# Motif terms of a convolution network: the large loads and stores move from SP's queue to GpSimd's

## The chip, the cores and the metric

One core of a Trainium2 chip runs the whole program. The metric is the device time in microseconds, the median of several executions. The engines are TensorE (PE), VectorE (DVE), ScalarE (ACT), GpSimd (POOL) and SyncE (SP). SP and GpSimd each issue DMA transfers, on queues of their own (q1 "hardware dynamic" and q0 "software dynamic" in the profile); 16 DMA engines serve both.

## The reference

For each of two images of 128 x 128 positions and 96 channels, a group-normalised copy of `x` goes through a channel attention (1x1 and 3x3 depthwise convolutions, softmax over channels), whose result is added to `x`. Then comes the part that matters here, on a group-normalised copy read as planes:

```
motif_nn = take_along_axis(motif, u_max[..., None, None], axis=3)   # one neighbour channel per (group, tap)
term = floor(motif * motif_nn * c_max[..., None, None] / Cg)
out_ser = motif * batch_mask + term          # batch_mask: 0 for image 0, 1 for image 1
...
for k in range(K * K):
    ki, kj = (k // K, k % K)
    out = out.at[:, :, :, ki:ki + Hm, kj:kj + Wm].add(ser2[:, :, :, k])
x = x + out
```

`motif` holds nine shifted views of each plane. The partner plane of a plane depends on data (`u_max`, by nearest neighbour over the Gram matrices), so it has to be gathered.

## The kernel before

The program runs per image: `attention`, `motif_grams` (normalise, write the planes `f` to DRAM, Gram matrices, partner choice) and `motif_terms` (from line 1028). Only `motif_terms` is changed. While it works on image 0 it also loads image 1 in pieces (`x_next`) and takes its statistics, since the next attention needs them.

`motif_terms` has the 128 planes on the partitions and works on N = 8 blocks of R = 16 rows. Per block there are nine tap steps (`sh` 0 to 8), in the order of `steps`: blocks go in pairs, and the steps of a pair alternate, (0,0), (1,0), (0,1), (1,1) and so on, so a pair takes 18 steps and an image 72. In this document product n, step n and move n carry the same number n from 0 to 71.

Per step, VectorE multiplies the plane's rows by the partner's rows (`product`, L1097, into `prod`); ScalarE rounds the scaled product (L1279, L1284); VectorE marks where rounding overshot (`overshoot`, L1213, two steps later); TensorE adds both into the accumulators in PSUM at the tap's shift (L1301, L1305). After a block's ninth tap `finish` (L1222) adds the accumulators to `x1c`. For image 1 `own_patches` (L1238) adds the block's own nine-fold patches at tap 3; for image 0 `stats_share` (L78) takes a share of the next image's statistics from step 19 on.

Transfers, with four buffers (`SLOTS`) each for fc, near, near2 and x1c:

- `fc<-f_planes` (`load_rows`, 768 KB): a block's planes. Blocks 0 and 1 at the start, block i+2 at tap 5 of block i.
- `x1c<-x_planes` (`load_rows`, 768 KB): the rows to which the result is added. Blocks 0 and 1 at tap 1, block i+2 at tap 4 of block i.
- `out<-x1c` (`store`, 768 KB): block i-2 at tap 2 of block i, the last two at the end, waited for at L1160.
- `x_next<-in_x` (`load_next`, 384 KB): 16 pieces, from step 7, four in every 13 steps, image 0 only.
- `near<-f_planes,index` (`gather`, L1166): the partner planes, by index from DRAM, two gathers per block (`near` for the first tap, `near2` for the partner's neighbour), issued by GpSimd. Those of blocks 0 and 1 at the start, those of block i+2 at taps 1 and 3 of block i.
- `near<-near` (L1137, about 100 KB): at each tap from 1 on one plane in eight gets a new partner, copied from near2 to near. The move of step n waits for product n-2 and, at tap 1, for the gather of near2; product n waits for it. These are the 128 moves of the run.

SP issues all of these but the gathers, from one written-out order: at each step the move first, then what else is due. GpSimd's own program has only two memsets and the gathers; the first four depend on the index that VectorE computes, the next four (blocks 2 and 3) wait for nothing, and later ones wait for the last products of the block whose buffer they take (L1077, through `product_made`). `on_pool` is False throughout, so GpSimd makes no product.

Of the kernel before, what the change touches and what calls it, by code (L numbers as in the profile page):

```python
# [33 lines left out]
B, H, W, C = 2, 128, 128, 96  # L34
# [10 lines left out]
KK = 9  # L45
# [7 lines left out]
QROWS = 32  # L53
NQ = H // QROWS
# [973 lines left out]
def motif_terms(nc, b, k, x, f_dram, x1_dram, out, gram_sems):  # L1028
# [3 lines left out]
    R = 16  # L1032
    N = H // R
    SLOTS = 4
# [3 lines left out]
    with ExitStack() as ctx:  # L1038
# [4 lines left out]
        fc = sb("fc", [P, SLOTS, R * C], F32)  # L1043
        x1c = sb("x1c", [P, SLOTS, R * C], F32)
# [4 lines left out]
        if b + 1 < B:  # L1049
            x_next = sb("x_next", [P, 2 * QROWS, C], F32)  # L1050
            next_in = [sem(f"next_in{j}_") for j in range(2)]
            next_stats = sem("next_stats")
# [9 lines left out]
        stored, near_in, near2_in, fc_in, x1_in = ([sem(f"{n}{j}_") for j in range(SLOTS)]  # L1062
                                                   for n in ("stored", "near_in", "near2_in", "fc_in", "x1_in"))
# [3 lines left out]
        number = {st: n for n, st in enumerate(steps)}  # L1067
        on_pool = [False for i, sh in steps]

        STATS_PER, STATS_AT, LOAD_AT = 13, 19, 7  # L1070
# [4 lines left out]
        def product_made(eng, n):  # L1075

            eng.wait_ge(prod_p if on_pool[n] else prod_v, sum(p == on_pool[n] for p in on_pool[:n + 1]))  # L1077

        def product_inputs(eng, n):

            i, sh = steps[n]
            s = i % SLOTS
            if sh == 0:
                eng.wait_ge(near_in[s], 16 * (i // SLOTS + 1))
                eng.wait_ge(fc_in[s], 16 * (i // SLOTS + 1))
                eng.wait_ge(edged, 2 if i == N - 1 else 1)
            else:
                eng.wait_ge(moved[i % 2], 16 * (8 * (i // 2) + sh))
            if n >= PRODS:
                eng.wait_ge(over_done, n - PRODS + 1)  # L1090

        def product(vec, n):
            i, sh = steps[n]
            s, (dy, dx) = i % SLOTS, TAPS[sh]
            fv = fc[:, s, :].rearrange("p (r c) -> p r c", c=C)[:, :, dx:dx + WM]
            nv = near[:, s, :].rearrange("p (r c) -> p r c", c=C)[:, 2 - dy:2 - dy + R, 0:WM]
            return vec.tensor_tensor(prod[:, n % PRODS], fv, nv, ALU.mult)  # L1097

        def run(i):

            a = (first_row(i) - (R * i - 2)) * C
            return slice(a, a + (last_row(i) - first_row(i)) * C + WM)

        out_p = out[b].rearrange("y x c -> y (x c)")
        block = ctx.enter_context(nc.Block())

        @block.sync
        def _(sp):
            def load_rows(dst, src, i, sem_):
                sp.dma_start(dst[:, i % SLOTS, :], src[:, R * i * C:(R * i + R) * C]).then_inc(sem_[i % SLOTS], 16)  # L1110

            def load_next(q, piece):

                cols, slot = QROWS // 4, QROWS * (q % 2)
                if q >= 2 and piece == 0:
                    sp.wait_ge(next_stats, q - 1)
                sp.dma_start(x_next[:, slot + cols * piece:slot + cols * (piece + 1), :],
                             x[b + 1][:, QROWS * q + cols * piece:QROWS * q + cols * (piece + 1), :]
                             ).then_inc(next_in[q % 2], 16)

            def store(i):
                sp.wait_ge(out_ready, i + 1)
                sp.dma_start(out_p[:, R * i * C:(R * i + R) * C], x1c[:, i % SLOTS, :]
                             ).then_inc(stored[i % SLOTS], 16)

            if b + 1 < B:
                for s_ in gram_sems.values():
                    sp.sem_clear(s_)
            for i in range(2):
                load_rows(fc, f_dram, i, fc_in)  # L1130
            for n, (i, sh) in enumerate(steps):
                if sh >= 1:

                    if sh == 1:
                        sp.wait_ge(near2_in[i % SLOTS], 16 * (i // SLOTS + 1))
                    product_made(sp, n - 2)
                    sp.dma_start(near[MC - sh:P:MC, i % SLOTS, run(i)], near2[MC - sh:P:MC, i % SLOTS, run(i)]  # L1137
                                 ).then_inc(moved[i % 2], 16)
                if sh == 5 and i + 2 < N:
                    if i >= 2:  # L1140
                        product_made(sp, number[(i - 2, KK - 1)])
                        product_made(sp, number[(i - 2, KK - 2)])
                        if b == 1:
                            sp.wait_ge(fold, i - 1)
                    load_rows(fc, f_dram, i + 2, fc_in)
                if i >= 2 and sh == 2:
                    store(i - 2)
                if sh == 1 and i < 2:
                    load_rows(x1c, x1_dram, i, x1_in)
                q, part = (n - LOAD_AT) // STATS_PER, (n - LOAD_AT) % STATS_PER  # L1150
                if b + 1 < B and 0 <= q < NQ and part in (0, 3, 6, 9):
                    load_next(q, part // 3)
                if sh == 4 and i + 2 < N:
                    if i >= 2:
                        sp.wait_ge(stored[(i + 2) % SLOTS], 16 * ((i + 2) // SLOTS))
                    load_rows(x1c, x1_dram, i + 2, x1_in)
            for i in range(N - 2, N):
                store(i)
            for j in range(SLOTS):
                sp.wait_ge(stored[j], 16 * (N // SLOTS))  # L1160

        @block.gpsimd
        def _(pool):
            def gather(i, second):
                s = i % SLOTS
                pool.indirect_dma_start(  # L1166
                    (near2 if second else near)[:, s, run(i)], None, f_dram.rearrange("y (e o) -> (y e) o", o=1),
                    bass.IndirectOffsetOnAxis(ap=index[:, second, i:i + 1], axis=0)
                ).then_inc((near2_in if second else near_in)[s], 16)


            nc.gpsimd.memset(near[:, 0, 0:2 * C], 0.0).then_inc(edged, 1)
            pool.wait_ge(indexed, 1)
            for second in range(2):
                gather(0, second)
                gather(1, second)
            for n, (i, sh) in enumerate(steps):
                if sh in (1, 3) and i + 2 < N:
                    if sh == 1 and i >= 2:
                        product_made(pool, number[(i - 2, KK - 1)])  # L1180
                        product_made(pool, number[(i - 2, KK - 2)])
                    if sh == 1 and i + 2 == N - 1:
                        nc.gpsimd.memset(near[:, (i + 2) % SLOTS, R * C:NR * C], 0.0).then_inc(edged, 1)
                    gather(i + 2, sh // 2)
                if on_pool[n]:
                    product_inputs(pool, n)
                    product(nc.gpsimd, n).then_inc(prod_p, 1)

        @block.vector
        def _(dve):  # L1190
# [172 lines left out]
```

## Time and profile before

| what | value |
|---|---|
| median of 3 runs | 1781.23 us (1780.07 to 1782.25) |
| the profiled execution, its own time | 1786.56 us |
| its span | 1784.6 us |
| PE busy | 1497.0 us (84%) |
| DVE busy | 990.3 us (55%) |
| ACT busy | 735.0 us (41%) |
| POOL busy | 317.9 us (18%) |
| granted TensorE clock, mean | 0.928 |
| q1 (SP's transfers) | 116.10 MB |
| q0 (GpSimd's transfers) | 27.49 MB |

All times of rows are microseconds from the span's start, in the one profiled execution. The shares are means over very different stages. The motif terms of image 0 run from about 608 to 908 us, those of image 1 from about 1485 to the end. An instruction of VectorE starts in the record while the one before it still drains, so neighbours overlap by some 0.1 us. In a timeline the square brackets hold the idle time ahead of an instruction and what ended it. A granted clock of 1.0 is 2.4 GHz, 0.5 is 1.2 GHz.

### The profile page before, as it was taken

To read this page: it belongs to the slowest core of one execution; us is meant where nothing else is said; L and a number is where in the kernel's file an instruction comes from. 1 tells how busy PE (TensorE), PEld (TensorE's weight loads), DVE (VectorE), ACT (ScalarE), POOL (GpSimd) and SP (SyncE) were. 2 spreads that over 40 slices of the span, in tenths; PEclk is the share of its full clock that TensorE was granted. 3 is DMA by queue.
4 is the path that set the end of the run, shared out by engine and by line. 5 is a ranking of instruction groups with operands and counts; after the bars stand their busy time and mean duration, and the time that the engine had idled before them with its cause. 6 is when DMAs were issued, how large, how long until landed. Compare 5 with 4: busy or idle time off the path is not lost. (4 is left out here: it accounts for less than half of the span.)

```text
span 1784.6 us, 40475 instructions
## 1 busy us (share of the span) xinstructions
PE 1497.0 (84%) x16955; PEld 1257.2 (70%) x16955; DVE 990.3 (55%) x1537; ACT 735.0 (41%) x769; POOL 317.9 (18%) x254
## 2 busy tenths in 40 slices
PE   0699999799299488988949999988975993898998
PEld 0699999699299344544539999988974991454554
DVE  7333332123743379999962333321346415999998
ACT  0133332100154178877812332330003532888886
POOL 2222222000531202100022222220005302024000
PEclk9999999899699689999979999998996996999999
DMA  5111111010003364462112222201010216362511
GB/s 190 35 35 34 37 35 28 13 74 38 36 2 143 116 234 166 151 215 74 38 63 60 61 60 59 61 16 49 38 73 1 85 61 234 99 198 78 169 59 52
DMA packets 50959, 145.99 MB, mean 82 GB/s; under 512 B 12311, under 2 KB 33421, under 8 KB 48143
## 3 DMA queue, kind: packets, MB, share of 16 engines
q1 hardware_dynamic: 46192, 116.10, 20.4%
q0 software_dynamic: 4608, 27.49, 4.3%
q8 instruction: 133, 2.18, 0.5%
q14 instruction: 26, 0.21, 0.0%
HBM read 72.69 MB, written 37.75 MB: 62 GB/s over the span
## 5 line engine op out<-in xcount | busy, mean ns | idle before, releaser
L1301 PE MATMUL acc<-rnd,ident 128*128 128x376 f32 x1152 | 405.5, 497 | 24.7 <-ACT rnd L1284 24.7
L599 PE MATMUL ps_a<-wa,xa 128*128 128x192 f16 x2304 | 406.2, 248 | 14.0 <-DMA xc<-low 14.0
L600 PE MATMUL ps_a<-wb,xb 128*128 128x192 f16 x2304 | 405.6, 248 | 0.0
L1301 PEld LDWEIGHTS acc<-rnd,ident 128*128 128x128 f32 x1152 | 224.6, 199 | 153.1 <-ACT rnd L1284 26.1
L1279 ACT ACTIVATE rnd_m<-prod,plus_round,scale 128x1504 f32<-128x1504 f32 x144 | 236.0, 1639 | 121.2 <-DVE prod L1097 114.8
L1097 DVE TENSOR_TENSOR prod<-fc,near 128x1504 f32<-128x1504 f32 x144 | 246.6, 1713 | 39.5 <-DMA near<-near 25.2
L1213 DVE SCALAR_TENSOR_TENSOR over<-prod,scale,rnd 128x1504 bf16<-128x1504 f32 x144 | 255.4, 1776 | 0.9 <-PE acc L1305 0.9
L599 PEld LDWEIGHTS ps_a<-wa,xa 128*128 128x128 f16 x2304 | 227.0, 99 | 15.5 <-issue 11.7
L468 DVE TENSOR_TENSOR qk<-ps_a,qk 128x384 f16<-128x384 f32 x128 | 71.4, 557 | 295.4 <-ACT squares L549 295.4
L1284 ACT ACTIVATE rnd<-rnd_m,minus_round 128x1504 f32<-128x1504 f32 x144 | 223.1, 1550 | 25.9 <-PE acc L1305 20.8
L600 PEld LDWEIGHTS ps_a<-wb,xb 128*128 128x128 f16 x2304 | 227.3, 99 | 1.0
L599 PE MATMUL ps_a<-wfa,xa 128*128 128x96 f16 x2232 | 220.1, 206 | 0.0
L600 PE MATMUL ps_a<-wfb,xb 128*128 128x96 f16 x2232 | 219.2, 206 | 0.0
L428 POOL TENSOR_TENSOR sq_sum<-sq_sum,squares 128x384 f32<-128x384 f32 x128 | 127.5, 996 | 408.9 <-ACT squares L549 408.9
L600 PEld LDWEIGHTS ps_a<-wfb,xb 128*128 128x128 f16 x2232 | 193.3, 98 | 0.1
L599 PEld LDWEIGHTS ps_a<-wfa,xa 128*128 128x128 f16 x2232 | 193.1, 98 | 0.0
L545 ACT ACTIVATE qk<-ps_a 128x384 f16<-128x384 f32 x128 | 62.9, 491 | 280.7 <-PE ps_a L602 280.7
L1305 PE MATMUL acc<-over,minus_ident 128*128 128x376 bf16 x576 | 119.1, 330 | 31.3 <-DVE over L1213 31.0
L516 DVE SCALAR_TENSOR_TENSOR img<-ps_a,img 128x384 f32 (+1 forms) x64 | 35.7, 557 | 179.8 <-PE ps_a L602 157.9
L1305 PEld LDWEIGHTS acc<-over,minus_ident 128*128 128x128 bf16 x576 | 50.1, 99 | 120.4 <-DVE over L1213 81.5
L127 ACT ACT_TABLE_LOAD x3 | 3.8, 1283 | 285.6 <-PEq L301 261.2
L951 DVE TENSOR_SCALAR turned_lo<-ps_m 126x768 f16<-126x768 f16 x102 | 56.4, 558 | 106.8 <-PE ps_m L855 106.8
(227 smaller groups left out, 2030.1 us busy)
## 6 DMA issues: line engine op xcount, KB each, us to landing
x_planes<-img SPq DMA_DIRECT2D x8, 1536.0 KB, 5.6
f_planes<-img SPq DMA_DIRECT2D x8, 1536.0 KB, 11.1
fc<-f_planes SPq DMA_DIRECT2D x16, 768.0 KB, 4.6
x1c<-x_planes SPq DMA_DIRECT2D x16, 768.0 KB, 4.8
out<-x1c SPq DMA_DIRECT2D x16, 768.0 KB, 3.3
near<-near SPq DMA_DIRECT2D x96, 107.9 KB, 2.2
xb<-xa SPq DMA_DIRECT2D x64, 97.5 KB, 2.1
img<-in_x SPq DMA_DIRECT2D x4, 1536.0 KB, 12.6
```

The lines of the kernel that those rows point to most:

```text
L428: nc.gpsimd.tensor_tensor(sq_sum[:, :], sq_sum[:, :], squares[:, s, :], ALU.add).then_inc(sq_added, 1)
L468: nc.vector.tensor_tensor(qk[:, s, :, 2 * C:4 * C], ps[s][:, 0:4 * C].rearrange("p (r o) -> p r o", r=2), qk[:, s, :, 0:2 * C], ALU.subtra ...
L545: nc.scalar.activation(qk[:, s, :, 0:2 * C], ps[s][:, 0:4 * C].rearrange("p (r o) -> p r o", r=2), ACT.Copy)
L599: nc.tensor.matmul(out, xa[:, row, dx:dx + W], wa[:, t, :], start=(t == 0), stop=False)
L600: nc.tensor.matmul(out, xb[:, row, dx:dx + W], wb[:, t, :], start=False, stop=False)
L951: last = nc.vector.tensor_scalar(columns(turned_lo[q % 2], col), six(ps_lo[u % 2]), 2.0, None, ALU.mult)
L1097: return vec.tensor_tensor(prod[:, n % PRODS], fv, nv, ALU.mult)
L1213: nc.vector.scalar_tensor_tensor(over[:, n % 2], prod[:, n % PRODS], scale[:, sh:sh + 1], rnd[:, n % RNDS], ALU.mult, ALU.is_lt).then_inc( ...
L1279: nc.scalar.activation(rnd_m[:, n % 2], prod[:, n % PRODS], ACT.Identity, bias=k["plus_round"][:, 0:1], scale=scale[:, sh:sh + 1]).then_in ...
L1284: nc.scalar.activation(rnd[:, n % RNDS], rnd_m[:, n % 2], ACT.Identity, bias=k["minus_round"][:, 0:1]).then_inc(rnd_done, 1)
L1301: nc.tensor.matmul(o(m), k["ident"][:, :], rnd[:, n % RNDS, BR * m:BR * m + BR, :], start=False, stop=False, skip_group_check=True)
L1305: last = nc.tensor.matmul(o(m), k["minus_ident"][:, :], over[:, n % 2, BR * m:BR * m + BR, :], start=False, stop=(sh == KK - 1), skip_grou ...
```

## The change

`load_rows`, `load_next` and `store` are moved, as they are, from the program of SP to that of GpSimd, with the calls of them. SP keeps the semaphore clears and the moves. GpSimd issues the first two fc loads ahead of its memset and its first gathers. In each step it now issues the gathers that are due, waits for product n-2, and then issues what SP issued behind its move. The waits for products that guarded the fc buffer's reuse are dropped for that one wait per step; the one for `fold` in image 1 stays. GpSimd waits for the last stores.

```diff
         @block.sync
         def _(sp):
-            def load_rows(dst, src, i, sem_):
-                sp.dma_start(dst[:, i % SLOTS, :], src[:, R * i * C:(R * i + R) * C]).then_inc(sem_[i % SLOTS], 16)
...
-            for i in range(2):
-                load_rows(fc, f_dram, i, fc_in)
             for n, (i, sh) in enumerate(steps):
...
-                if sh == 5 and i + 2 < N:
-                    if i >= 2:
-                        product_made(sp, number[(i - 2, KK - 1)])
-                        product_made(sp, number[(i - 2, KK - 2)])
-                        if b == 1:
-                            sp.wait_ge(fold, i - 1)
-                    load_rows(fc, f_dram, i + 2, fc_in)
-                if i >= 2 and sh == 2:
-                    store(i - 2)
-                if sh == 1 and i < 2:
-                    load_rows(x1c, x1_dram, i, x1_in)
...
-                if sh == 4 and i + 2 < N:
-                    if i >= 2:
-                        sp.wait_ge(stored[(i + 2) % SLOTS], 16 * ((i + 2) // SLOTS))
-                    load_rows(x1c, x1_dram, i + 2, x1_in)
-            for i in range(N - 2, N):
-                store(i)
-            for j in range(SLOTS):
-                sp.wait_ge(stored[j], 16 * (N // SLOTS))
 
         @block.gpsimd
         def _(pool):
...
+            for i in range(2):
+                load_rows(fc, f_dram, i, fc_in)
             nc.gpsimd.memset(near[:, 0, 0:2 * C], 0.0).then_inc(edged, 1)
             pool.wait_ge(indexed, 1)
...
                     gather(i + 2, sh // 2)
-                if on_pool[n]:
-                    product_inputs(pool, n)
-                    product(nc.gpsimd, n).then_inc(prod_p, 1)
+                if n >= 2:
+                    product_made(pool, n - 2)
+                if sh == 5 and i + 2 < N:
+                    if b == 1 and i >= 2:
+                        pool.wait_ge(fold, i - 1)
+                    load_rows(fc, f_dram, i + 2, fc_in)
+                if i >= 2 and sh == 2:
+                    store(i - 2)
+                if sh == 1 and i < 2:
+                    load_rows(x1c, x1_dram, i, x1_in)
+                q, part = (n - LOAD_AT) // STATS_PER, (n - LOAD_AT) % STATS_PER
+                if b + 1 < B and 0 <= q < NQ and part in (0, 3, 6, 9):
+                    load_next(q, part // 3)
+                if sh == 4 and i + 2 < N:
+                    if i >= 2:
+                        pool.wait_ge(stored[(i + 2) % SLOTS], 16 * ((i + 2) // SLOTS))
+                    load_rows(x1c, x1_dram, i + 2, x1_in)
+            for i in range(N - 2, N):
+                store(i)
+            for j in range(SLOTS):
+                pool.wait_ge(stored[j], 16 * (N // SLOTS))
```

## Rows read from the trace of the kernel before

**Rows 1.** Busy time by stretch: start and steady state of image 0; granted clock, DMA share, GB/s last

```profile
608.00:650.00 42.00, 21.48 (x59) 11.31 (x60) 21.78 (x26) 19.83 (x13) 10.09 (x9) 0.65 0.71 263
650.00:716.00 66.00, 61.48 (x222) 34.91 (x221) 66.00 (x51) 57.35 (x37) 11.32 (x4) 0.95 0.57 183
```

**Rows 2.** Waits of VectorE, whole run: total, times, longest

```profile
DVE prod L1097 <- DMA near<-near: 25.2, 7, 6.5
```

**Rows 3.** Timeline of VectorE, start of image 0: products 2, 3, 4 and 5

```profile
628.54 1.73 DVE L1097 TENSOR_TENSOR prod<-fc,near 128x1504 f32<-128x1504 f32 x1 [6.38 <-DMA near<-near]
...
633.99 1.73 DVE L1097 TENSOR_TENSOR prod<-fc,near 128x1504 f32<-128x1504 f32 x1 [2.03 <-DMA near<-near]
...
640.77 1.73 DVE L1097 TENSOR_TENSOR prod<-fc,near 128x1504 f32<-128x1504 f32 x1 [3.36 <-DMA near<-near]
...
644.11 1.72 DVE L1097 TENSOR_TENSOR prod<-fc,near 128x1504 f32<-128x1504 f32 x1
```

**Rows 4.** Timeline of SP's queue, start of image 0

```profile
610.22 0.80 SPq L1110 DMA_DIRECT2D fc<-f_planes  x2
622.47 0.60 SPq L1137 DMA_DIRECT2D near<-near  x1
623.13 0.56 SPq L1110 DMA_DIRECT2D x1c<-x_planes  x1
624.77 0.55 SPq L1137 DMA_DIRECT2D near<-near  x1
625.37 0.57 SPq L1110 DMA_DIRECT2D x1c<-x_planes  x1
```

**Rows 5.** DMA issues between 608 and 626: count, size, us to landing

```profile
x1c<-x_planes SPq DMA_DIRECT2D x2, 768.0 KB, 12.4
...
near<-near SPq DMA_DIRECT2D x1, 107.9 KB, 9.2
near<-near SPq DMA_DIRECT2D x1, 95.9 KB, 6.0
```

**Rows 6.** DMA issues of the whole run: median us to landing

```profile
x1c<-x_planes SPq DMA_DIRECT2D x16, 768.0 KB, 4.8
...
near<-near SPq DMA_DIRECT2D x96, 107.9 KB, 2.2
```

**Rows 7.** Busy time by stretch, two short stretches at image 0's start

```profile
612.00:618.00 6.00, 0.00 (x0) 0.00 (x0) 0.00 (x0) 0.00 (x0) 4.47 (x6) 0.50 0.98 403
...
636.00:642.00 6.00, 5.68 (x18) 2.97 (x17) 2.64 (x2) 2.94 (x2) 0.00 (x0) 0.90 0.46 156
```

**Rows 8.** Timeline of VectorE, image 1: products 2, 3, 4, and one at 1660

```profile
1504.47 1.73 DVE L1097 TENSOR_TENSOR prod<-fc,near 128x1504 f32<-128x1504 f32 x1 [6.51 <-DMA near<-near]
...
1509.88 1.73 DVE L1097 TENSOR_TENSOR prod<-fc,near 128x1504 f32<-128x1504 f32 x1 [1.99 <-DMA near<-near]
...
1515.65 1.72 DVE L1097 TENSOR_TENSOR prod<-fc,near 128x1504 f32<-128x1504 f32 x1 [2.35 <-DMA near<-near]
...
1660.68 1.72 DVE L1097 TENSOR_TENSOR prod<-fc,near 128x1504 f32<-128x1504 f32 x1 [2.62 <-DMA near<-near]
```

**Rows 9.** Timelines of GpSimd, then of VectorE beside its gathers

```profile
609.13 0.26 POOL L1172 MEMSET near<- 128x192 f32 x1 [53.57 <-POOLq L730]
...
613.67 0.94 POOL L1166 DMA_INDIRECT near<-f_planes,index  x1 [0.30 <-issue]
...
1565.91 3.03 POOL L1166 DMA_INDIRECT near<-f_planes,index  x1 [0.30 <-issue]
...
1628.75 15.57 POOL L1166 DMA_INDIRECT near<-f_planes,index  x1 [53.15 <-DVE prod L1097]
...
1568.05 1.78 DVE L1213 SCALAR_TENSOR_TENSOR over<-prod,scale,rnd 128x1504 bf16<-128x1504 f32 x1
...
1643.40 1.77 DVE L1222 TENSOR_TENSOR x1c<-x1c,acc 128x1536 f32<-128x1536 f32 x1
```

**Rows 10.** Timeline of SP's queue: the last two stores

```profile
1777.71 3.50 SPq L1123 DMA_DIRECT2D out<-x1c  x2
```

More of the change, by code:

```diff
@@ L1108, in _ @@
         def _(sp):
-            def load_rows(dst, src, i, sem_):
-                sp.dma_start(dst[:, i % SLOTS, :], src[:, R * i * C:(R * i + R) * C]).then_inc(sem_[i % SLOTS], 16)
[L1112 to L1124, printed above, removed]
             if b + 1 < B:
@@ L1138, in _ @@
                                  ).then_inc(moved[i % 2], 16)
-                if sh == 5 and i + 2 < N:
-                    if i >= 2:
-                        product_made(sp, number[(i - 2, KK - 1)])
-                        product_made(sp, number[(i - 2, KK - 2)])
-                        if b == 1:
-                            sp.wait_ge(fold, i - 1)
-                    load_rows(fc, f_dram, i + 2, fc_in)
-                if i >= 2 and sh == 2:
-                    store(i - 2)
-                if sh == 1 and i < 2:
-                    load_rows(x1c, x1_dram, i, x1_in)
-                q, part = (n - LOAD_AT) // STATS_PER, (n - LOAD_AT) % STATS_PER
-                if b + 1 < B and 0 <= q < NQ and part in (0, 3, 6, 9):
-                    load_next(q, part // 3)
-                if sh == 4 and i + 2 < N:
-                    if i >= 2:
-                        sp.wait_ge(stored[(i + 2) % SLOTS], 16 * ((i + 2) // SLOTS))
-                    load_rows(x1c, x1_dram, i + 2, x1_in)
-            for i in range(N - 2, N):
-                store(i)
-            for j in range(SLOTS):
-                sp.wait_ge(stored[j], 16 * (N // SLOTS))
         @block.gpsimd
@@ L1169, in gather, with load_rows, load_next, store @@
                 ).then_inc((near2_in if second else near_in)[s], 16)
+            def load_rows(dst, src, i, sem_):
+                pool.dma_start(dst[:, i % SLOTS, :], src[:, R * i * C:(R * i + R) * C]).then_inc(sem_[i % SLOTS], 16)
+            def load_next(q, piece):
+                cols, slot = QROWS // 4, QROWS * (q % 2)
+                if q >= 2 and piece == 0:
+                    pool.wait_ge(next_stats, q - 1)
+                pool.dma_start(x_next[:, slot + cols * piece:slot + cols * (piece + 1), :],
+                             x[b + 1][:, QROWS * q + cols * piece:QROWS * q + cols * (piece + 1), :]
+                             ).then_inc(next_in[q % 2], 16)
+            def store(i):
+                pool.wait_ge(out_ready, i + 1)
+                pool.dma_start(out_p[:, R * i * C:(R * i + R) * C], x1c[:, i % SLOTS, :]
+                             ).then_inc(stored[i % SLOTS], 16)
+            for i in range(2):
+                load_rows(fc, f_dram, i, fc_in)
             nc.gpsimd.memset(near[:, 0, 0:2 * C], 0.0).then_inc(edged, 1)
```

## The prediction

> **What bounds the kernel now.** The change touches one stage, the motif terms of each image, so I first asked the busy time by stretch how that stage runs. In steady state VectorE has no free time: 66.00 us of 66.00, and two of its products stand 3.34 us apart (640.77 to 644.11) [rows 1, 3]. In the first 42 us it is busy for only 21.78 us [rows 1]. The list of waits says on what: 25.2 us in 7 waits for a small move `near<-near`, the largest single releaser in the stage [rows 2]. So a gain can only come from those 25.2 us, a loss from anything that makes VectorE wait anew, or that lengthens a start or an end, where nothing covers it.
>
> The VectorE timeline of image 0 places three of the seven waits, before products 2, 3 and 4 (step numbers of the kernel): 6.38, 2.03 and 3.36 us [rows 3]. The SP timeline shows what lies between the moves: each of the first two is followed at once by a 768 KB load of x1c on the same queue [rows 4]. The DMA issues of this stretch give the landing times: 6.0 us for the first move, 9.2 for the second, and 12.4 for x1c loads that take 4.8 us in the whole run's median, where a move takes 2.2 [rows 5, 6]. The engines' share of busy time is 0.98 early in it, and only after 636 us does it fall to 0.46 [rows 7]: everything issued before that shares full DMA engines. Image 1 repeats the pattern (6.51, 1.99, 2.35 us) and has a seventh wait of 2.62 us at 1660 [rows 8].
>
> **The change, part by part.** Of SP's queue, 64 transfers go: 16 fc, 16 x1c, 16 stores and 16 x_next pieces, with their waits. SP keeps the 128 moves. GpSimd gets the 64 behind and between its 32 gathers, and a new wait at each step, for product n-2.
>
> *Moves 3 and 4 at the start.* Now move 3 stands behind x1c(0) and move 4 behind x1c(0) and x1c(1) in SP's queue. Afterwards SP's queue holds moves alone. GpSimd's queue holds fc(0), fc(1), four gathers, the fifth gather, x1c(0), the sixth gather, x1c(1); the gathers seven and eight now wait until step 6. Before product 4 that is 10 large transfers instead of 12, and the two taken out are the last. At some 2.1 us each (860 KB at the 403 GB/s of a full stretch [rows 7]) ten last 21 us, until about 633; move 4 is issued at the end of product 2, near 630, and product 4 needs it at 635. I take both later waits as gone: product 4 then follows product 2 by two steps of 3.33 us, at 628.54 + 6.66 = 635.2 instead of 640.77, **-5.6 us**; in image 1 at 1504.47 + 6.66 = 1511.1 instead of 1515.65, **-4.5 us** [rows 3, 8]. Bounds: 0 if moves wait as long as now, -10.1 for both. What is late next here is TensorE: its granted clock is 0.50, the 1.2 GHz level, before its first work of the stage, and 0.65 in the mean of the stretch [rows 1, 7]; I leave 1 us for that in the range.
>
> *Move 2* waits first for its gather and then 6.0 us for itself, with nothing ahead of it on its own queue [rows 4, 5]. What held it was the other queue's gathers, and those stand ahead of it still. I take 0; if its own queue being empty were to help, it could gain 6.0 - 2.2 = 3.8 us per image, 7.6 in all.
>
> *The wait at 1660.* GpSimd's gather of 1628.75 took 15.57 us, until VectorE's instruction at 1643.40 [rows 9], so three more gathers fell into 5 us, with two stores, and a move came late. After the change a wait for a product stands between gathers, so that they come a step apart. **-2.6 us**; 0 if the bunch forms again.
>
> *Starts.* GpSimd makes descriptors for 0.94 us before a transfer can begin (the undisturbed gather), SP's issue of a load returns in 0.57 [rows 4, 9]. In image 0 SP begins at 610.22, GpSimd at 609.13 already, and the two loads put 2 x 1.24 = 2.5 us of issuing ahead of the first gather, whose data stand behind these loads in any case: -0.2 us. In image 1, where SP doesn't clear semaphores first, +0.8. Together **+0.6 us**; bounds 0 and +2.5 (the gathers each 1.24 us later).
>
> *Ends.* Each image ends with a store whose landing nothing covers: issued at about 1780.9, with the end at 1784.6 [rows 10]. From GpSimd it starts about 0.9 us later (0.94 us of descriptors). Twice: **+1.8 us**, bounds 0.8 and 4. The Trainium skill (DMA: Bandwidth & Descriptors, Latency and other measured facts) has 1 us to the first byte from GpSimd against 0.6 from SP; by that the two ends would cost 0.8.
>
> *Steady state.* GpSimd gets 64 x (0.94 + 0.30) = 79 us of issuing over the two stages, SP loses about 35; neither is the bound. What hides it: per pair of blocks, 18 steps or 60 us and more, GpSimd has at most 10 large issues and, in image 0, some five x_next pieces. At the 3.03 us that a gather takes beside VectorE [rows 9] fifteen are 45 us. The tightest is fc, issued 8 steps (27 us) before its product. Behind each new wait for product n-2 stand later gathers: gather(4) is issued after product 17 and wanted at step 36, 19 steps. A store waits for VectorE's sum and holds the next issues for some 3 us; the x1c slot is wanted two steps behind. I take 0. If the cover goes, the price is in the third rival.
>
> Sum: -5.6 - 4.5 - 2.6 + 0.6 + 1.8 = -10.3 us. Against the profiled execution, 1786.56 us with a span of 1784.6, that is 1776.3. It ran 5.3 us above the median of the runs; on the median, 1781.23 - 10.3 = **1771 us**.
>
> **The rivals.**
>
> *More than forecast.* Move 2 is also set free: 7.6 us more, 1763 us. For it: its queue holds nothing else. Against: it holds nothing ahead of it now either.
>
> *Nothing.* The engines, not the queue, hold the moves; x1c(0) and x1c(1) on GpSimd's queue hold moves 3 and 4 just as long, and the bunch at 1660 forms again. Left are starts and ends: 1781.2 + 2.4 = 1783.6, within what a measurement of this kernel can tell from no change (0.2%, 3.6 us). For it: the share of 0.98, and move 2's 6.0 us. Against: move 3 took 3.2 us longer than move 2, with only a load of its own queue between them [rows 5].
>
> *Slower: GpSimd is held off by VectorE.* The gather of 15.57 us shows that this can be: it ended 0.92 us after VectorE began an instruction that reads the accumulators in PSUM (1643.40), while others ended about 0.9 us after a change of VectorE instruction (1568.94, with `over` begun at 1568.05) [rows 9]. So a gather wants a gap between VectorE's instructions with two inputs in SBUF, and sometimes gets none; the 0.9 us of descriptors then run beside them. Such a gather now has loads behind it. It decides when the delay reaches the 27 us of fc less about 5 for landing. In image 1 a gather at tap 3 could be held until VectorE runs dry of fc; then each pair costs about what a load takes behind a backlog, 12.4 us [rows 5], three pairs 37 us: 1771 + 37 = 1808. Against: eight gathers amid such streams took 3 to 4 us each, one 15.57; a direct load has no index to read; and the short own-patch instructions of image 1, one to four steps on, leave gaps. The Trainium skill (SBUF — State Buffer, SBUF: two separate sides) warns of just this: DMAs from GpSimd starve where VectorE holds the shared port. It names copies in fast modes for descriptors, and two-input instructions for GpSimd's reads; the rows agree with the second.
>
> **How the numbers follow.** The forecast has 0.60 (own range 1765 to 1777: the wait at 1660 may stay, TensorE may take 1 us, starts and ends may cost 3 more). More than forecast 0.12, nothing 0.14, slower 0.14, since loads from GpSimd beside this VectorE stream are in no row. The range takes the first three, 1763 to 1784. Faster by over 0.2%: 0.60 + 0.12 = 0.72; within: 0.14; slower: 0.14.
>
> **What the changed profile would show.** Right: waits of `prod` for `near<-near` fall from 25.2 us in 7 to about 12.9 in 2, both before product 2; moves 3 and 4 land within 7 us; the last store ends about 0.9 us later behind its sum. Wrong: VectorE waiting before products 3 and 4 as now; a wait of `prod` for `fc<-f_planes` or of `x1c` for `x1c<-x_planes`; direct issues on GpSimd of over 3 us; a move late in steady state behind a load.

## The result, and the profile after

The changed kernel takes 1784.01 us (median of 20 runs, 1781.34 to 1786.41) where the kernel before takes 1781.37 (20 runs, 1776.41 to 1784.56). The ratio is 1.0016, with an interval from 1.0009 to 1.0022: 2.6 us slower, less than the 3.6 us that I had named as telling from no change, but with 1 outside the interval. The forecast was 10 us faster. The median lies at the upper end of the range that the prediction gave, 1763 to 1784 us, and 0.01 us outside it, and the likeliest case is wrong.

The page of the changed kernel, its span, queues and DMA issues (q1 is fed by SP, q0 by GpSimd; the issues end with median us to landing):

```profile
span 1782.5 us, 40529 instructions
...
q1 hardware_dynamic: 36976, 72.06, 13.1%
q0 software_dynamic: 12800, 71.54, 11.6%
...
fc<-f_planes POOLq DMA_DIRECT2D x16, 768.0 KB, 5.5
x1c<-x_planes POOLq DMA_DIRECT2D x16, 768.0 KB, 5.9
out<-x1c POOLq DMA_DIRECT2D x16, 768.0 KB, 3.8
near<-near SPq DMA_DIRECT2D x96, 107.9 KB, 2.3
```

The change does what it says: loads and stores are GpSimd's, SP keeps the moves. Busy time by stretch of the changed kernel, the two stretches of [rows 1] with the same columns, and the waits of VectorE, total, times and longest:

```profile
608.00:650.00 42.00, 25.47 (x79) 13.90 (x80) 27.49 (x28) 25.76 (x17) 15.08 (x17) 0.71 0.85 299
650.00:716.00 66.00, 61.00 (x227) 35.18 (x225) 64.37 (x55) 56.16 (x36) 14.73 (x16) 0.97 0.56 181
```

```profile
DVE prod L1097 <- DMA near<-near: 16.8, 6, 6.7
DVE prod L1097 <- DMA near<-f_planes,index: 14.9, 4, 7.3
DVE part L88 <- PEq L1038: 9.0, 1, 9.0
```

VectorE is busy for 27.49 us of the first 42 where it was 21.78 [rows 1], and waits for moves for 16.8 us where it waited 25.2 [rows 2]. In the steady stretch it has lost what it had: 64.37 us of 66.00, where it was 66.00. And a third line has grown that had no part in the prediction: one wait of 9.0 us, in front of line 88, the first VectorE instruction behind the stage of image 0. In the kernel before this wait is 3.8 us.

The timeline of VectorE in the changed kernel, start of image 0 (products 2 to 5), answers to [rows 3]:

```profile
627.87 1.73 DVE L1097 TENSOR_TENSOR prod<-fc,near 128x1504 f32<-128x1504 f32 x1 [6.27 <-DMA near<-near]
...
631.21 1.72 DVE L1097 TENSOR_TENSOR prod<-fc,near 128x1504 f32<-128x1504 f32 x1
...
634.57 1.73 DVE L1097 TENSOR_TENSOR prod<-fc,near 128x1504 f32<-128x1504 f32 x1
...
637.91 1.72 DVE L1097 TENSOR_TENSOR prod<-fc,near 128x1504 f32<-128x1504 f32 x1
```

The waits before products 3 and 4 are gone and the one before product 2 stands as it was. Counted from the VectorE instruction that begins the stage (609.17 before, 608.45 after), product 4 begins at 26.12 us instead of 31.60, 5.5 earlier; in image 1 at 26.14 instead of 29.69, 3.55 earlier.

Now the end of image 0. Timeline of VectorE in the changed kernel: the last sum and the next instruction; then the timeline of GpSimd, its last store and its next instruction; then the rows of the block's end (line 1038) in this image, with count, shortest/median/longest ns and start:

```profile
902.27 1.75 DVE L1218 TENSOR_TENSOR x1c<-x1c,acc 128x1536 f32<-128x1536 f32 x1 [1.41 <-PE acc L1301]
913.06 0.49 DVE L88 TENSOR_REDUCE part<-stats 128x32 f32<-128x256 f32 x1 [9.03 <-PEq L1038]
```

```profile
904.32 0.53 POOL L1145 DMA_DIRECT2D out<-x1c  x1 [2.34 <-DVE x1c L1218]
913.02 0.53 POOL L396 MEMSET low<- 96x520 uint32 x1 [8.17 <-POOLq L1038]
```

```profile
L1038 POOLq DRAIN  x1: 4644/4644/4644, 908.1 to 908.1; - x1
```

The same places in the kernel before: the rows of line 1038 (both images) and VectorE's wait:

```profile
L1038 POOLq DRAIN  x2: 13791/21728/29665, 755.6 to 1631.9; - x2
...
L1038 SPq DRAIN  x2: 7/7/7, 911.0 to 1784.4; - x2
```

```profile
911.23 0.49 DVE L88 TENSOR_REDUCE part<-stats 128x32 f32<-128x256 f32 x1 [3.82 <-PEq L1038]
```

Every engine ends a block with a DRAIN, and the block is over when the last one is. Before, SP waited for the last landing and its own DRAIN took 7 ns; GpSimd's was long, 13.8 and 29.7 us, but began at 755.6 and 1631.9, over a hundred microseconds ahead of the end. Now GpSimd waits for the last landing, until 908.1, and then its DRAIN runs for 4.64 us with nothing beside it. The end of image 0 is 9.03 us instead of 3.82, the end of image 1 (end of the last sum to end of the span) 1782.5 - 1774.55 = 7.95 instead of 1784.6 - 1780.84 = 3.76.

**The ledger of the two profiled executions.** Stage start to the end of the last sum: image 0 from 298.24 to 295.57 us (-2.7), image 1 from 294.88 to 289.97 (-4.9). The two ends: +5.2 and +4.2. Together +1.8 us, which agrees with the 2.6 of the medians. (The two spans alone would say -2.1; but between them lie stretches that the change doesn't touch and that differ by 3.9 us, which is why I go by the stage.)

Of the 5.5 us that image 0 wins in its first four steps, 2.8 are lost again on the way. The timeline of VectorE in the changed kernel has these two waits, which stood nowhere before, and the timeline of GpSimd shows what lies ahead of the first:

```profile
711.88 1.72 DVE L1097 TENSOR_TENSOR prod<-fc,near 128x1504 f32<-128x1504 f32 x1 [1.63 <-DMA near<-near]
...
783.67 1.73 DVE L1097 TENSOR_TENSOR prod<-fc,near 128x1504 f32<-128x1504 f32 x1 [1.01 <-DMA near<-near]
```

```profile
699.18 0.53 POOL L1145 DMA_DIRECT2D out<-x1c  x1 [4.71 <-DVE x1c L1218]
699.70 0.55 POOL L1139 DMA_DIRECT2D x_next<-in_x  x1
700.55 1.05 POOL L1125 DMA_INDIRECT near<-f_planes,index  x1 [0.30 <-issue]
701.91 1.38 POOL L1125 DMA_INDIRECT near<-f_planes,index  x1 [0.30 <-issue]
```

A store that waits for VectorE's sum holds up what stands behind it, and then four large transfers leave within 4 us. That looks like the cause of the late moves; the experiment that was to show it didn't (below).

### The profile page after: what moved, and what is told of

Same layout as the page of the kernel before. It is cut to its first block and busy times, and to the rows that moved or that the text cites. A ratio compares the mean times of both kernels' runs of the same rounds, so it can differ in the third digit from the quotient of the medians.

```text
span 1782.5 us, 40529 instructions
## 1 busy us (share of the span) xinstructions
PE 1491.0 (84%) x16955; PEld 1253.3 (70%) x16955; DVE 990.3 (56%) x1537; ACT 735.3 (41%) x769; POOL 337.5 (19%) x318
## 5 line engine op out<-in xcount | busy, mean ns | idle before, releaser
L1097 DVE TENSOR_TENSOR prod<-fc,near 128x1504 f32<-128x1504 f32 x144 | 246.8, 1714 | 31.7 <-DMA near<-near 16.8
```

## The experiments

**What makes the end long.** There are three other ways of sharing the last two stores and the landing wait between SP and GpSimd; the rest of the changed kernel stays. First, both on SP (`last_store_sp` is `store` with a semaphore of its own, `last_stored`).

```diff
@@ changed kernel, SP, at its end
+            for i in range(N - 2, N):
+                last_store_sp(i)
+            for j in range(SLOTS):
+                sp.wait_ge(stored[j], 16 * (N // SLOTS - (j >= SLOTS - 2)))
+            sp.wait_ge(last_stored, 32)
@@ GpSimd, at its end
-            for i in range(N - 2, N):
-                store(i)
-            for j in range(SLOTS):
-                pool.wait_ge(stored[j], 16 * (N // SLOTS))
```

> The changed kernel, but the last two stores of each image and the wait for their landing are SP's again. By the profile of the changed kernel the time from the end of the last x1c sum to the next work grew at both image ends (3.82 to 9.04 us, and 3.76 to 7.95 us to the end of the span), 9.4 us together, where 1.8 was forecast. Theory A (GpSimd, once it has issued a DMA late, comes some 4 to 5 us late to the end of its block): both ends fall back to about 3.8 us and the kernel is 9.4 us faster than the changed one, about 6.8 us (0.4%) faster than before. Theory B (waiting for the landing on GpSimd is what is slow): the same here. Rival C (the changed kernel lost its start's gain in the steady state, the ends are an accident of one profile): within 2 us of the changed kernel.

Measured: 1774.16 us (1771.88 to 1775.39, 5 runs) against 1781.34 of the kernel before, ratio 0.9955, interval 0.9942 to 0.9967. That is 9.9 us less than the changed kernel. The rows of line 1038 and VectorE's wait behind image 0 in this kernel:

```profile
L1038 POOLq DRAIN  x2: 3170/3826/4481, 886.2 to 1752.0; - x2
...
L1038 SPq DRAIN  x2: 7/7/7, 907.6 to 1772.6; - x2
```

```profile
907.88 0.49 DVE L88 TENSOR_REDUCE part<-stats 128x32 f32<-128x256 f32 x1 [3.81 <-PEq L1038]
```

GpSimd's DRAIN is as long as ever, but begins at 886.2 and 1752.0, some 20 us ahead of the end. Both ends are back at 3.81 and 3.74 us. So all of the loss lies in the last two stores and their wait, and the rest of the change is worth -7.2 us.

The other two take one of the two parts each: the stores on GpSimd and the wait on SP, and the stores on SP and the wait on GpSimd.

```diff
@@ changed kernel, GpSimd, at its end
             for i in range(N - 2, N):
                 store(i)
-            for j in range(SLOTS):
-                pool.wait_ge(stored[j], 16 * (N // SLOTS))
@@ SP, at its end
+            for j in range(SLOTS):
+                sp.wait_ge(stored[j], 16 * (N // SLOTS))
```

> The changed kernel, GpSimd still issues the last two stores, but the wait for their landing is SP's. Theory A (GpSimd's late DMA itself holds GpSimd at the end of its block): the ends stay at about 9 and 8 us, the time is the changed kernel's within 1.5 us. Theory B (only GpSimd's wait for the landing is slow): the ends fall to about 4.7 us (3.8 and 0.9 for GpSimd's start of a DMA), 7.6 us faster than the changed kernel.

```diff
@@ changed kernel, SP, at its end
+            for i in range(N - 2, N):
+                last_store_sp(i)
@@ GpSimd, at its end
-            for i in range(N - 2, N):
-                store(i)
             for j in range(SLOTS):
-                pool.wait_ge(stored[j], 16 * (N // SLOTS))
+                pool.wait_ge(stored[j], 16 * (N // SLOTS - (j >= SLOTS - 2)))
+            pool.wait_ge(last_stored, 32)
```

> The changed kernel, the last two stores issued by SP, but GpSimd waits for their landing. Theory A (a late DMA of its own is what holds GpSimd): the ends fall to about 3.8 us, 9 us faster than the changed kernel. Theory B (GpSimd's wait for the landing is slow): the ends stay at 8 us or so, at most 2 us faster than the changed kernel.

Measured: stores on GpSimd, wait on SP 1779.47 us (11 runs, ratio 0.9990, 0.9981 to 0.9999), ends 6.44 and 5.73 us; stores on SP, wait on GpSimd 1782.74 (12 runs, ratio 1.0013, 0.9998 to 1.0028), ends 8.33 and 6.95. Line 1038 in the one, then in the other:

```profile
L1038 POOLq DRAIN  x2: 5226/5554/5882, 904.9 to 1773.5; - x2
L1038 SPq DRAIN  x2: 7/7/7, 908.7 to 1777.2; - x2
```

```profile
L1038 SPq DRAIN  x2: 122/122/123, 903.6 to 1774.3; - x2
L1038 POOLq DRAIN  x2: 3170/3826/4481, 906.7 to 1777.4; - x2
```

The kernel whose last stores SP issues, and for which only GpSimd waits, is nearly as slow as the changed one. Its ends exceed the 3.82 and 3.76 of before by 4.51 and 3.19 us, its DRAINs are 4.48 and 3.17: the whole excess is the DRAIN. It isn't the issue of the store, nor the wait in itself, but what GpSimd must still do once the wait is over. That refutes a store of GpSimd's own as the cause. With the wait on SP the DRAIN starts while the store is still under way (904.9), and part of it is covered. It is longer there than in the changed kernel, 5.88 and 5.23 us instead of 4.64 and 3.33, so the ends fell to 6.44 and 5.73 us and not to the 4.7 that was expected if the wait alone were slow.

**If it is the DRAIN, one more of them, placed earlier, should take it away** with every store and wait left on GpSimd:

```diff
@@ changed kernel, GpSimd, at its end
+            pool.drain()
             for i in range(N - 2, N):
                 store(i)
```

> The changed kernel with one more DRAIN on GpSimd, ahead of its last two stores of each image, where it waits for VectorE anyway. So far the DRAIN that ends GpSimd's block took 4.644 us in an image with 56 DMAs issued by GpSimd, 4.481 with 54, 3.988 with 48, 3.333 with 40, 3.170 with 38 and 2.680 with 32: 0.082 us for each DMA since the block began. Theory E (the DRAIN pays 0.082 us for each DMA since the last DRAIN): the last DRAIN falls to about 0.2 us, the ends from 9.03 and 7.95 us to about 4.6 and 4.8, and the kernel is some 7.5 us faster than the changed one, near 1776.5. Rival (a fixed cost of leaving a block late, or one by the whole block's DMAs): ends and time stay as in the changed kernel.

Measured: 1774.70 us (1773.56 to 1777.34, 6 runs) against 1782.06, ratio 0.9967, 0.9954 to 0.9979; some 2 us better than expected. Line 1038 and VectorE's wait:

```profile
L1038 POOLq DRAIN  x2: 214/215/216, 908.3 to 1773.4; - x2
```

```profile
908.79 0.49 DVE L88 TENSOR_REDUCE part<-stats 128x32 f32<-128x256 f32 x1 [4.61 <-PEq L1038]
```

The DRAIN ahead of the stores takes 4.48 and 3.17 us beside the last steps, the one at the end 0.21. One added line wins 9.3 us of the 9.9. What is left of the ends, 4.61 - 3.82 - 0.21 = 0.6 us and 4.85 - 3.76 - 0.21 = 0.9 us, is what a store from GpSimd costs beyond one from SP; the changed kernel gives the same from its own rows (9.03 - 3.82 - 4.64 = 0.57 and 7.95 - 3.76 - 3.33 = 0.86).

**And the kernel before should slow down** if nothing but the landing wait moves to GpSimd. It issues only 16 gathers an image.

```diff
@@ kernel before, SP, at its end
-            for j in range(SLOTS):
-                sp.wait_ge(stored[j], 16 * (N // SLOTS))
@@ GpSimd, at its end
+            for j in range(SLOTS):
+                pool.wait_ge(stored[j], 16 * (N // SLOTS))
```

> The kernel before, only the wait for the last stores' landing at the end of each image is GpSimd's in place of SP's. GpSimd issues its 16 gathers per image and nothing else. Theory E: the DRAIN behind the wait takes 16 x 0.082 + 0.06 = 1.4 us, so both ends grow from 3.8 to 5.2 us, 2.8 us in all (0.16%). Rival (a fixed cost of 3.3 to 4.6 us): 7 to 8 us slower.

Measured: 1783.87 us (12 runs) against 1782.06, ratio 1.0011, 1.0000 to 1.0022: +1.8 us where 2.8 was expected. Its rows say more than its time:

```profile
L1038 POOLq DRAIN  x2: 1365/1368/1372, 911.1 to 1781.2; - x2
```

```profile
912.76 0.49 DVE L88 TENSOR_REDUCE part<-stats 128x32 f32<-128x256 f32 x1 [5.22 <-PEq L1038]
```

The end of image 0 grew by 1.40 us, that of image 1 by 1.70 (1782.8 - 1777.34 = 5.46 us, where it was 3.76); the DRAINs are 1.37. Where all of GpSimd's transfers have landed before it begins, its length goes by the number of DMAs that GpSimd has issued in the block since its last DRAIN:

| DMAs by GpSimd | in | DRAIN, us |
|---|---|---|
| 56 | changed kernel, image 0 | 4.644 |
| 54 | last stores on SP, image 0 | 4.481 |
| 48 | all stores on SP, image 0 | 3.988 |
| 40 | changed kernel, image 1 | 3.333 |
| 32 | all stores on SP, image 1 | 2.680 |
| 16 | kernel before with the wait moved | 1.37 |
| 2 | DRAIN ahead of the last stores | 0.215 |

From 16 to 56 it is (4.644 - 1.37) / 40 = 0.082 us for each, in every row to 0.01 us. It goes by their number and not by their bytes: the 16 DMAs that image 0 has more than image 1 are x_next pieces of 384 KB, and the 6 between 54 and 48 are stores of 768 KB.

**What the moving of the stores did in mid-stage.** All stores and their wait go back to SP; loads and x_next stay on GpSimd. If stores that wait for a sum make the bunches, the new waits should go.

```diff
@@ changed kernel, GpSimd
-                if i >= 2 and sh == 2:
-                    store(i - 2)
@@ SP, behind the move
+                if i >= 2 and sh == 2:
+                    store_sp(i - 2)
...
```

> The changed kernel with all stores, and the last wait, on SP; GpSimd keeps the loads and gathers. As with the last stores alone the ends come back to 3.8 us. On top of it theory D: in the middle GpSimd waited for the x1c sums ahead of its stores, so that two stores, a piece of x_next and two gathers went out within 3 us, and moves behind them came late (waits of 1.63 and 1.01 us in image 0, 0.56 and 0.64 in image 1). By D these waits go and the time is 1 to 4 us below that with only the last stores on SP. Rival: the stores weigh on the moves from SP's queue too, or SP's wait for the sum holds its moves; then no difference or slower by 1 to 2 us.

Measured: 1772.72 us (1768.57 to 1782.59, 12 runs), ratio 0.9961, 0.9944 to 0.9977; 1.4 us below the kernel with only the last stores on SP, which the two intervals don't tell apart. The mid-stage waits didn't go: 17.4 us in 7 waits for moves, with five of 0.56 to 1.57 us behind the first of each image. So the bunches that a store waiting in GpSimd's queue makes aren't needed for a move to come late; where exactly a late move meets which transfer is left open.

**Where the gain at the start comes from.** The change does two things there at once: it takes x1c(0) and x1c(1) out of SP's queue, and, by the new wait for product n-2, it holds back the gathers that nobody needs yet. Each alone, in the kernel before. First the wait alone, no DMA changes its engine:

```diff
@@ kernel before, GpSimd, in each step behind its gathers
-                if on_pool[n]:
-                    product_inputs(pool, n)
-                    product(nc.gpsimd, n).then_inc(prod_p, 1)
+                if n >= 2:
+                    product_made(pool, n - 2)
```

> The kernel before, only GpSimd waits at each step for product n-2, so that the gathers of blocks 2 and 3 leave later; all loads and stores stay SP's. Theory Q (moves 3 and 4 come late since x1c loads stand before them on SP's queue): products 3 and 4 still wait, together over 3 us per image; at most 2 us gained per image at the start. Theory W (they come late since all 12 transfers share full engines; two fewer free them): product 4 comes about 4 us earlier in each image. In both the bunch of gathers at 1645 to 1650 goes, with its wait of 2.6 us.

Then the queue, without a wait at each step (`x1_first` are semaphores of these two loads' own, for which VectorE waits in the place of `x1_in`):

```diff
@@ kernel before, SP
-                if sh == 1 and i < 2:
-                    load_rows(x1c, x1_dram, i, x1_in)
@@ GpSimd, behind its gathers
+                if sh == 1 and i < 2:
+                    product_made(pool, i)
+                    pool.dma_start(x1c[:, i, :], x1_dram[:, R * i * C:(R * i + R) * C]).then_inc(x1_first[i], 16)
```

> The kernel before, only the x1c loads of blocks 0 and 1 are GpSimd's (after product 0 and 1), between its gathers; the gathers of blocks 2 and 3 do not wait for products otherwise. So SP's queue holds moves alone up to product 4, and GpSimd's all 12 large transfers. Theory Q: the waits before products 3 and 4 go, 5.6 and 4.5 us are gained, 1771. Theory W: the moves share the engines with twelve transfers as before, and less than half of that comes.

And the two together:

> The kernel before with both parts that act at the start: GpSimd waits at each step for product n-2, and the x1c loads of blocks 0 and 1 are GpSimd's. All else, stores and later loads too, stays SP's, and GpSimd's block ends early. The wait alone gave 9.2 us (1772.84 beside 1782.06). What is left to gain at the start are its waits of 0.32 and 0.49 us before product 3: so 1772 us, the same as with the wait alone within 1 us, if the two parts relieve the same thing. If they were independent terms the sum would be 9.2 + 6.0, 1767.

Measured: wait alone 1772.84 us (5 runs) against 1782.06, ratio 0.9951, 0.9938 to 0.9964; queue 1776.02 (6 runs), ratio 0.9967, 0.9954 to 0.9980; both 1772.50 (5 runs) against 1780.48, ratio 0.9956, 0.9943 to 0.9969. That is -9.2, -6.0 and -8.0 us: they don't add up. The kernel with the wait alone, waits of VectorE and its timeline at products 2, 3 and 4:

```profile
DVE prod L1097 <- DMA near<-near: 14.2, 4, 6.7
```

```profile
629.18 1.72 DVE L1097 TENSOR_TENSOR prod<-fc,near 128x1504 f32<-128x1504 f32 x1 [6.72 <-DMA near<-near]
...
632.92 1.73 DVE L1097 TENSOR_TENSOR prod<-fc,near 128x1504 f32<-128x1504 f32 x1 [0.32 <-DMA near<-near]
...
636.26 1.72 DVE L1097 TENSOR_TENSOR prod<-fc,near 128x1504 f32<-128x1504 f32 x1
```

With x1c(0) and x1c(1) ahead of moves 3 and 4 on SP's queue still, the wait before product 3 falls from 2.03 us [rows 3] to 0.32 and the one before product 4 is gone. The wait at 1660 [rows 8] is gone too, since the gathers now come one step apart. Product 4 begins 4.9 and 3.8 us sooner from the start of the stage, as expected if full engines were the cause. The wait alone, a change of three lines, gives all that moving 64 transfers gave, and no long end. In the queue run product 4 begins 27.45 us from the start of the stage instead of 31.60, product 5 waits for another 1.26 us, and a wait of 2.23 us stays at 1653. This run isn't quite the queue alone: the two loads wait for products 0 and 1, and so do the gathers behind them. The sixth to eighth leave 4.1 to 5.6 us later in the stage than before (the sixth at 620.90 - 608.59 = 12.31 us, before at 617.41 - 609.17 = 8.24). What the queue does by itself is therefore not separated. On top of the wait it adds nothing that these runs can tell, as expected if both relieve the same thing.

**Can the rest of the start be had?** The next three keep every load and store on SP, take over the wait for product n-2 on GpSimd, and space the transfers out. In the first, on top of the wait, x1c(0) and x1c(1) leave one tap later:

```diff
-                if sh == 1 and i < 2:
+                if sh == 2 and i < 2:
                     load_rows(x1c, x1_dram, i, x1_in)
```

> The kernel before with GpSimd's wait for product n-2, and the x1c loads of blocks 0 and 1 issued by SP one tap later (behind move 4 and move 5 in place of behind moves 2 and 3). No DMA changes its engine. Expected the same as with both parts on GpSimd, 1772 us: moves 3 and 4 have an empty queue, and fewer bytes are before them. If GpSimd's queue were what helps, this stays at or above the wait alone (1772.8).

Measured: 1774.51 us (6 runs) against 1780.48, ratio 0.9967, 0.9955 to 0.9979. No better than the wait alone: products 3 and 4 have no wait in image 0, but image 1 has one of 0.96 us at 1514.60 and one of 0.19 behind it, and image 0 four of 0.18 to 0.73 later on.

In the second, the gathers issued in the steps of the first two blocks (those of blocks 2 and 3) also wait for the product of their own step, so that only the fourth gather of the start still stands ahead of move 2:

```diff
+                    if i < 2:
+                        product_made(pool, n)
                     gather(i + 2, sh // 2)
```

> As the run without GpSimd's loads, and the first gathers of blocks 2 and 3 wait for the product of their own step, so that the fifth gather leaves behind product 2 and not before product 0. If move 2 waits (6.7 us of VectorE's time in each image) because the fourth and fifth gather stand before it on the DMA engines, it now passes one transfer less: product 2 comes about 2.1 us earlier in each image, 4 us in all, 1768 us. If a move waits for something else (its own latency, the 16 rows it copies), no difference.

Measured: 1776.34 us (10 runs) against 1780.48, ratio 0.9974, 0.9964 to 0.9983, worse than without. Waits of VectorE, and the DMA issues between 608 and 628 with us to landing, in this kernel:

```profile
DVE prod L1097 <- DMA near<-near: 18.1, 11, 2.9
```

```profile
near<-near SPq DMA_DIRECT2D x2, 95.9 KB, 2.2
near<-near SPq DMA_DIRECT2D x1, 107.9 KB, 2.2
```

Moves 2 to 4 now land in 2.2 us, where move 2 took 6.0 [rows 5] and takes 6.2 in image 1 of the changed kernel; the wait before product 2 falls from 6.5 to 2.9 us. But seven new ones of 0.3 to 2.45 us follow within image 0, and two of 1.77 and 1.25 in image 1. The reading is that the gathers held back meet the loads that follow, and the moves between them.

The third tries that reading and spaces all of it. In the first two blocks the gather of tap 1 waits for the product of its own step, the others for product n-2; x1c(0) and x1c(1) leave at tap 4, the next x1c at tap 5, the next fc at tap 6.

```diff
-                if sh == 5 and i + 2 < N:
+                if sh == (5 if i >= 2 else 6) and i + 2 < N:
...
-                if sh == 1 and i < 2:
+                if sh == 4 and i < 2:
...
-                if sh == 4 and i + 2 < N:
+                if sh == (4 if i >= 2 else 5) and i + 2 < N:
...
+                    if i < 2:
+                        product_made(pool, n if sh == 1 else n - 2)
                     gather(i + 2, sh // 2)
```

> The kernel before with GpSimd's wait for product n-2, every load and store still SP's, and the first pair's transfers spaced so that about one large one leaves behind each product: gathers of blocks 2 and 3 behind products 2, 3, 4 and 5, x1c(0) and x1c(1) behind products 6 and 7, x1c(2) and (3) behind 8 and 9, fc(2) and (3) behind 10 and 11. In the run with later gathers the wait before product 2 fell from 6.5 to 2.9 us, as expected, but a gather and an x1c load then left behind the same product and 7 to 10 us of new waits came at products 5 to 12. If collisions of two large transfers behind one product are what makes a move late, the early product 2 (3.5 us in each image beside the wait alone) is now kept: 1766 us, 0.85% below before. If any gather in these steps delays a move, the gain goes again and the time is 1772 or more. Own patches of image 1 want x1c(0) two steps after it leaves; at worst 1 to 3 us wait there.

Measured: 1766.44 us (1765.79 to 1769.24, 6 runs) against 1781.03, ratio 0.9926, 0.9911 to 0.9941: as expected, and 14.6 us faster than the kernel before. Waits of VectorE and the timeline at products 2 and 3:

```profile
DVE prod L1097 <- DMA near<-near: 7.3, 4, 2.9
```

```profile
623.57 1.73 DVE L1097 TENSOR_TENSOR prod<-fc,near 128x1504 f32<-128x1504 f32 x1 [2.90 <-DMA near<-near]
...
626.91 1.72 DVE L1097 TENSOR_TENSOR prod<-fc,near 128x1504 f32<-128x1504 f32 x1
```

Of the 25.2 us of waits for moves [rows 2] 7.3 are left, and the ends are 3.82 and 3.80 us as before.

## Why the prediction was wrong

**Ends: the step that failed.** The prediction priced them at +1.8 us, with bounds 0.8 and 4, as "a store whose landing nothing covers", begun 0.9 us later. The store's own lateness was right: 0.57 and 0.86 us. What was missed is GpSimd's DRAIN behind it: 4.64 + 3.33 = 8.0 us. The ends cost 9.4. The change puts GpSimd in the place of the last engine to arrive, and I had looked at what that engine issues, not at what it does to leave the block. The rows stood in the trace of the kernel before, two DRAINs of 13.8 and 29.7 us on GpSimd against 7 ns on SP. They cost nothing there because they began early. Of the 12.1 us between the forecast of -10.3 and the ledger's +1.8 the ends are 7.6, the steady state with the wait at 1660 is 4.1, and the starts are 0.4.

**Steady state: taken at 0, and the wait at 1660 at -2.6 us.** The wait fell from 2.62 to 0.64 us, as argued. But new ones of 1.63, 1.01 and 0.56 us came in. Waiting for moves behind product 4 grew from 2.62 to 3.84 us in all, and together the two steps cost 1.5 us instead of winning 2.6. The reason given for 0 looked at GpSimd's time alone (large issues done well before their data are wanted), and not at what the transfers in flight do to a move. GpSimd's issues come in fours within 4 us; that these bunches are the cause isn't shown.

**Moves 3 and 4: right in size, less so in cause.** Product 4 was forecast two steps of 3.33 us behind product 2, 5.6 and 4.5 us sooner than before. It follows it after 634.57 - 627.87 = 6.70 us instead of 12.23 [rows 3], and after 1510.72 - 1504.06 = 6.66 in image 1 instead of 11.18 [rows 8]: -5.5 and -4.5. The argument had two legs: the moves' own queue is free, and two gathers less stand ahead of product 4. The runs speak for the second: with the gathers held back and the queue as it was, the time falls by 9.2 us (the wait at 1660 among them), and with the queue freed as well by 8.0. The queue run gives -6.0, but it holds three gathers back too, so what the first leg is worth by itself stays open.

**Starts: right within some tenths.** From the start of the stage to product 2 it was 19.37 us in image 0 and 18.51 in image 1, and is 19.42 and 19.48: +1.0 us where +0.6 was forecast, nearly all in image 1 as argued.

**Move 2: right.** Taken at 0; 6.38 us before, 6.27 after, 6.51 and 6.67 in image 1. It was held by gathers on the other queue: the run that holds back the fifth and those behind it lands it in 2.2 us. So the rival of more than forecast (an empty queue would free it) is refuted: the queue was never what held it.

**Slower by starvation: refuted.** The page of the changed kernel has no direct issue held: on GpSimd's timeline they take 0.53 to 0.59 us, beside VectorE's two-input products, and no gather takes more than 3.36 us, where one took 15.57 [rows 9]. I had reckoned with 0.94 for a direct issue. The Trainium skill (SBUF — State Buffer, SBUF: two separate sides) counts an instruction with two SBUF inputs as a lock only against a GpSimd operation that reads SBUF; the trace agrees, with 0.53 us for a load that has no index to read, and 0.94 to 3.36 us for gathers, which have one. The forecast had a slower case with the right sign and the wrong mechanism.

**Nothing: the time came out near its 1783.6 us, but not its reasons.** It had the moves held as long as now; they weren't. A gain of some 7.5 us and a loss of 9.4 cancelled, by luck. Without the cause of the second, the run would read as "the change does nothing", and with it one added line makes it a gain of 7 us.

The sum with the measured terms: -5.5 - 4.5 for moves 3 and 4, +1.0 for the starts, +9.4 for the ends, and +1.5 for what happens behind product 4 (+2.8 in image 0, -1.4 in image 1), is +1.8 us on the profiled executions, +2.6 on the medians.

## What to carry to other kernels

At each end of a block look which engine arrives last, and at its DRAIN's row: GpSimd's has a length that goes by the DMAs it has issued, and it is free only while another engine is still at work. Let SP issue or at least await the last stores, or drain GpSimd ahead of them. Where a small urgent move is late, ask first which large transfers are in flight that nobody needs yet, on any queue, and hold these back one step apart; another queue for the large ones gets the move past some of them only.

## What the runs showed of the hardware

GpSimd's DRAIN costs 0.082 us for each DMA that it has issued since the block's start or its last DRAIN, 4.64 us for 56. This holds where its transfers have landed before it begins. In the kernel before, with only 16 gathers an image, its rows are 13.8 and 29.7 us long. They begin at 755.6 and 1631.9, when some of the gathers haven't been issued yet: the last ones are issued at 760.28 and 1649.61 and land 8.4 and 11.2 us later, at 768.7 and 1660.8. The DRAINs end at 769.4 and 1661.6, 0.7 and 0.8 us behind these landings. In the run with the first x1c loads on GpSimd they end 0.8 us behind the last landing in both images (767.0 and 1655.2). So all four last until GpSimd's own transfers have landed. With the same gathers and the DRAIN behind the landing wait it took 1.37 us. With a store still under way when it begins it took 5.88 us for 56 DMAs and 5.23 for 40; how that is made up no run tells.

Move 2, on an otherwise empty queue, landed in 6.0 to 6.3 us in the kernel before, in image 1 of the changed kernel and with the wait alone, where a move's median is 2.2 [rows 6]. In the kernel before it was issued at 622.47, when the fourth to seventh gather had been issued on the other queue (614.92 to 618.65). It landed at 628.5, behind the fourth and the fifth (624.7 and 627.6) and ahead of the sixth and the seventh (631.7 and 636.2). With the fifth held back it landed in 2.2 us, though the fourth was still under way (issued at 614.64, landed at 624.5). So a queue of its own gets a move past part of the other queue's backlog and not past all of it. The Trainium skill (DMA: Bandwidth & Descriptors, Queues, rings and completion order) says that each DMA engine takes turns between queues, a packet of some 9 to 17 descriptors at a time. The trace agrees in that the move passes two gathers issued before it. No run here shows where a turn ends; with descriptors of some 6 KB, 16 engines and the 403 GB/s of [rows 7], a turn would be an estimated 2 to 4 us, as long as what the move loses here, 3.8 to 4.1.

A direct DMA takes GpSimd 0.53 to 0.59 us to issue, about as long as SP's 0.55 to 0.60 [rows 4], even beside VectorE's streams.
